# Two cross-attention layers on one Trainium2 core: units of 256 queries, keys and values projected once per batch, layer 1 fourteen groups behind

## What is computed

```python
# layer 0: text tokens 0..1019, image tokens 1020..1023
q = heads(x @ W_q)
k_t, v_t = heads(text @ W_k), heads(text @ W_v)
probs_t = softmax(q @ k_t.T * scale)
text_out = probs_t @ v_t
attn_scores = q @ heads(ip @ W_k_ip).T * scale
qsem = l2norm(probs_t @ text)              # 512 columns for every head
sem = qsem @ l2norm(ip).T
probs_ip = softmax(attn_scores + 0.5 * sem) * spatial_mask
x1 = (text_out + probs_ip @ v_ip) @ W_out + b_out + x

# layer 1: text tokens 0..76, image tokens 77..1023
out = (attend(q, text) + attend(q, image)) @ Wo + bo + x1
```

## Time and profile before

| | us |
|---|---|
| median of three runs | 3646.74 (3644.2 to 3650.6) |
| the profiled execution's own time | 3650.53 |
| its span, first to last instruction | 3648.7 |
| TensorE busy (matmuls) | 3440.8 |
| VectorE, ScalarE, GpSimd busy | 2018.2, 1638.5, 824.4 |
| mean granted TensorE clock | 0.975 |

### The profile page before, as it was taken

The page is one execution under the profiler, slowest core; times in us unless marked ns, Lnnn a source line. Parts: engine busy times, 40 slices in busy tenths (PEclk is TensorE's granted clock), DMA queues, the critical chain, the costliest instruction groups (busy, mean ns, idle before and its releaser), DMA issues.

```text
span 3648.7 us, 58131 instructions
## 1 busy us (share of the span) xinstructions
PE 3440.8 (94%) x21896; PEld 2650.6 (73%) x21896; DVE 2018.2 (55%) x4648; ACT 1638.5 (45%) x3628; POOL 824.4 (23%) x648
## 2 busy tenths in 40 slices
PE   6999999999999999999999999999999999877887
PEld 3788999997888887777777777777688877633333
DVE  4544444453444455655555565655555565656986
ACT  0233434442332345444454454444444554534876
POOL 2111000101101122222222221212221121234665
PEclk8999999999999999999999999999999999988999
DMA  4220111112252111131451111213143111139221
GB/s 157 56 82 25 50 35 28 36 27 82 53 63 71 45 52 50 33 93 36 59 98 43 46 48 50 52 32 88 39 53 37 26 32 33 25 99 79 55 52 33
DMA packets 391741, 196.67 MB, mean 54 GB/s; under 512 B 296972, under 2 KB 355164, under 8 KB 391458
## 3 DMA queue, kind: packets, MB, share of 16 engines
q1 hardware_dynamic: 391464, 192.96, 24.8%
HBM read 136.68 MB, written 55.44 MB: 53 GB/s over the span
## 4 chain that ended last, share of the span: by engine, by line
PE 81%; DVE 6%; ACT 5%; DMA 3%; issue 2%; POOL 2%; SPq 1%; POOLq 0%; ACTq 0%; DVEq 0%
PE acc L783 9%; PE acc L776 9%; PE acc L778 8%; PE acc L779 8%; PE acc L784 8%; PE acc L777 7%; PE av L817 3%; PE spare L853 3%; ACT prob L958 2%; PE spare L817 2%; PE acc L810 2%; PE acc L808 2%; PE score L741 2%; PE score L736 2%; PE score L743 2%
## 5 line engine op out<-in xcount | busy, mean ns | idle before, releaser
L958 ACT ACTIVATE prob<-score 128x512 f32<-128x512 f32 x1280 | 799.4, 625 | 1642.4 <-PE score L743 1241.7
L776 PE MATMUL acc<-tok_v,prob_hi 128*128 128x300 f32 x2240 | 873.4, 390 | 11.8 <-DVE v_f L1083 3.7
L961 ACT ACTIVATE prob_hi<-score 128x512 fp32r<-128x512 f32 x1280 | 799.9, 625 | 0.0
L783 PE MATMUL acc<-tok_v,prob_lo 128*128 128x278 f32 (+1 forms) x2560 | 746.9, 292 | 7.3 <-DVE prob_lo L1021 7.3
L778 PE MATMUL acc<-tok_lo,prob_hi 128*128 128x256 f32 (+1 forms) x2560 | 742.5, 290 | 0.0
L779 PE MATMUL acc<-tok_lo,prob_hi 128*128 128x256 f32 (+1 forms) x2560 | 720.5, 281 | 0.0
L784 PE MATMUL acc<-tok_v,prob_lo 128*128 128x256 f32 (+1 forms) x2560 | 719.5, 281 | 0.0
L1021 DVE TENSOR_TENSOR prob_lo<-prob,prob_hi 128x512 fp32r<-128x512 f32 x880 | 653.0, 743 | 96.7 <-ACT prob_hi L961 95.7
L1255 POOL TENSOR_TENSOR prob_lo<-prob,prob_hi 128x512 fp32r<-128x512 f32 x400 | 529.9, 1338 | 730.5 <-ACT prob_hi L961 729.5
L777 PE MATMUL acc<-tok_v,prob_hi 128*128 128x256 f32 x2240 | 629.2, 281 | 0.0
L778 PEld LDWEIGHTS acc<-tok_lo,prob_hi 128*128 128x128 f32 (+1 forms) x2560 | 485.3, 190 | 10.4 <-issue 9.6
(11 more groups left out here) (221 smaller groups left out, 4438.9 us busy)
## 6 DMA issues: line engine op xcount, KB each, us to landing
k_ring<-k_scr SPq DMA_DIRECT2D x480, 64.0 KB
ctx_t<-in_ctxT SPq DMA_DIRECT2D x8, 2048.0 KB, 10.8
q_ring<-q_scr SPq DMA_DIRECT2D x480, 32.0 KB
v_scr<-v_stage SPq DMA_DIRECT2D x32, 440.0 KB, 2.5
tok_v<-v_scr SPq DMA_DIRECT2D x80, 176.0 KB, 3.3
k_scr<-part_bf SPq DMA_DIRECT2D x32, 384.0 KB, 2.5
v_scr<-v_stage SPq DMA_DIRECT2D x36, 330.0 KB, 9.2
v_ring<-v_scr SPq DMA_DIRECT2D x80, 148.5 KB, 3.3
```

Source lines behind the costliest of these rows:

```text
L776: e.matmul(out_a[:, 0:SEG + VCOLS], p_hi, tok_v[0:kk, c, seg, v_lo:v_lo + SEG + VCOLS], start=first, stop=False)
L783: e.matmul(out_a[:, v_one:v_one + SEG + VH], p_lo, tok_v[0:kk, c, seg, v_lo + v_one:v_lo + v_one + SEG + VH], start=False, stop=False)
L958: e.activation(prob[:, es, :], bank_s[:, :], ACT.Exp, scale=SCALE)
L961: e.activation(prob_hi[:, ps, :], bank_s[:, :], ACT.Exp, scale=SCALE).then_inc(s_exp, 1)
```

## The change

A batch's 512 queries are cut in two units of 256 (PARTS = 2), in both layers: 16 units, 160 groups of 8 chunks. A chunk is 256 keys by 256 queries in both layers. Keys and values are projected once per batch by `project_kv`, a job of its own beside the jobs of the queries (`project_q`); `job_tasks` keeps one job of each kind under way. LAYER_LAG is 14 of the smaller groups. The tiles of the closing get memory of their own. The constants of order (LOOK_LOAD 3, LOOK_MAX 2, AHEAD 3, RING 4, the DMAs of a group) stay.

```diff
-LAYER_LAG = 17
+LAYER_LAG = 14
-B, SQ, D, E, T = 4, 512, 320, 512, 1024
+BATCHES, PARTS = 4, 2
+B, SQ, D, E, T = BATCHES * PARTS, 512 // PARTS, 320, 512, 1024
-PER_GROUP = GROUP * NT
+UNIT_KEYS = 2
+NU = NT // UNIT_KEYS
+PER_GROUP = GROUP * NU
...
-    def project(u):
+    def project_q(u):
         def loads():
-            o.note["loads", u] = (done["x_in"], done["w"], done["ctx"], tuple(done["xout"]))
-            o.add("loads", u)
+            o.note["q_loads", u] = (done["x_in"], tuple(done["xout"]))
+            o.add("q_loads", u)
...
+        return [loads] + [(NM, q_task(m)) for m in range(NM)]
+
+    def project_kv(u):
+        layer = UNITS[u][0]
+
+        def loads():
+            o.note["kv_loads", u] = (done["w"], done["ctx"])
+            o.add("kv_loads", u)
+        tasks = [loads]
...
         for m in range(NM):
-            tasks.append((NM, q_task(m)))
             tasks += [(NE * (1 + (half == (0 if layer else 1))), k_task(m, half)) for half in range(2)]
...
         if layer == 0:
-            add_job(rest + project(B + b), place[(B + b, 0)] - LOOK_LOAD)
+            add_job(rest + project_q(B + b), place[(B + b, 0)] - LOOK_LOAD)
             if b + 2 < B:
-                add_job(project(u + 2), place[(u + 2, 0)] - LOOK_LOAD)
+                add_job(project_q(b + 2), place[(b + 2, 0)] - LOOK_LOAD)
+            if b % PARTS == 1 and b + 3 < B:
+                add_job(project_kv(b + 3), place[(b + 3, 0)] - LOOK_LOAD, "kv")
+            if b % PARTS == 0 and b + 2 < B:
+                add_job(project_kv(B + b + 2), place[(B + b + 2, 0)] - LOOK_LOAD, "kv")
...
         while jobs and (quota > 0 or min(jobs, key=lambda x: x[0])[0] <= g):
-            if under_way and under_way[0] in jobs:
-                job = under_way[0]
-            else:
-                job = min(jobs, key=lambda x: x[0])
-                under_way[:] = [job]
+            first = {}
+            for x in sorted(jobs, key=lambda x: x[0]):
+                first.setdefault(x[2], under_way.get(x[2], x))
+            job = min(first.values(), key=lambda x: x[0])
+            under_way[job[2]] = job
...
-        slots = PER_GROUP * ST - 4 if layer == 0 else PER_GROUP
+        slots = PER_GROUP * 2 * UNIT_KEYS - 4 if layer == 0 else PER_GROUP
...
-                    if UNITS[u][0] == 1:
-                        e.matmul(score[n % 2][:, :], k_ring[0:depth, slot, j, c * P:(c + 1) * P],
-                                 q_ring[0:depth, slot, j, :], start=True, stop=True).then_inc(s_score, 1)
...
+                    queries = q_ring[0:depth, slot, j, :]
+                    e.matmul(score[n % 2][:, 0:SQ], k_ring[0:depth, slot, j, 2 * c * P:(2 * c + 1) * P],
+                             queries, start=True, stop=True)
+                    e.matmul(score[n % 2][:, SQ:2 * SQ], k_ring[0:depth, slot, j, (2 * c + 1) * P:(2 * c + 2) * P],
+                             queries, start=True, stop=True).then_inc(s_score, 1)
...
-                    e.matmul(both[0:n_out, :], weights, prob_hi[:, ps, :], start=first, stop=False, skip_group_check=not first)
+                    for k in range(UNIT_KEYS):
+                        e.matmul(both[0:n_out[k], 0:SQ], weights[k], prob_hi[:, ps, queries[k]],
+                                 start=r == 0 and k == 0, stop=False, skip_group_check=r > 0 or k > 0)
                     e.wait_ge(s_low[on_pool[n]], low_nth[n])
-                    e.matmul(both[0:n_out, :], weights, prob_lo[:, ps, :], start=False, stop=first or last, skip_group_check=not first).then_inc(s_main, 1)
+                    for k in range(UNIT_KEYS):
+                        mm = e.matmul(both[0:n_out[k], 0:SQ], weights[k], prob_lo[:, ps, queries[k]], start=False,
+                                      stop=r == 0 and k == 0 or r == NU - 1 and k == 1, skip_group_check=r > 0 or k > 0)
+                    mm.then_inc(s_main, 1)
...
+        FUSED, TURNED = HS * IP, NM * SQ
+        closing = sb("closing", [P, FUSED + SQ + 2 * TURNED])
```

More of the change, by code:

```diff
@@ L95, in plan @@
     groups = len(seq)
-    chunks = [(g, u, gi * GROUP + j, c) for g, (u, gi) in enumerate(seq) for j in range(GROUP) for c in range(NT)]
+    chunks = [(g, u, gi * GROUP + j, c) for g, (u, gi) in enumerate(seq) for j in range(GROUP) for c in range(NU)]
     now = [0]
     later, urgent, bgq, current = deque(), deque(), deque(), []
-    done = dict(part=[0, 0], splits=0, vst=0, xout=[0, 0], ctx=-1, x_in=-1, w=-1)
+    done = dict(part=[0, 0], splits=0, vst=0, xout=[0] * NM, ctx=-1, x_in=-1, w=-1)
     def settle():
@@ L114, in lower @@
             done["part"][i % 2] += 1
-            o.note["qk", u, m] = tuple(done["part"])
+            o.note[key[0] + "_split", u, m] = tuple(done["part"])
         later.append((now[0] + 2, lower))
-    def project(u):
-        layer, b = UNITS[u]
-        tasks = []
+    def project_q(u):
         def loads():
-            o.note["loads", u] = (done["x_in"], done["w"], done["ctx"], tuple(done["xout"]))
-            o.add("loads", u)
-        tasks.append(loads)
+            o.note["q_loads", u] = (done["x_in"], tuple(done["xout"]))
+            o.add("q_loads", u)
         def q_task(m):
@@ L239, in residual @@
         def residual(m):
-            settle()
-            o.note["residual", u, m] = (done["part"][m % 2], tuple(done["xout"]))
             o.add("residual", u, m)
-        tasks += [lambda: residual(0), lambda: residual(1)]
+        tasks += [lambda m=m: residual(m) for m in range(NM)]
         tasks += [(ST + 1 if layer == 0 else 1, turn(m)) for m in range(NM)]
@@ L254, in go @@
                         yield
[L255 to L258, removed]
+                done["xout"][m] += 1
             return go
@@ L297, in turn_head @@
         o.add("turn_head", u, h)
-    first_unit = project(0)
-    first_loads, first_qk, first_v_loads, *first_v = (first_unit[0], first_unit[1:1 + 3 * NM], *first_unit[1 + 3 * NM:])
+    q_loads, *first_q = project_q(0)
+    kv_loads, *first_kv = project_kv(0)
+    first_k, first_v_loads, first_v = first_kv[:2 * NM], first_kv[2 * NM], first_kv[2 * NM + 1:]
+    first_qk = [t for m in range(NM) for t in (first_q[m], first_k[2 * m], first_k[2 * m + 1])]
     o.add("row_const")
-    first_loads()
+    q_loads()
+    kv_loads()
     o.add("row_scr")
@@ L344, in job_tasks @@
         total, rate = 0, 0
-        for d, tasks in sorted(jobs, key=lambda x: x[0]):
+        for d, tasks, _ in sorted(jobs, key=lambda x: x[0]):
             total += steps_of(tasks)
@@ L642, in cross_attention_pair @@
         s_iprep = sem("ip_rep_done")
-        unit_nth = {s[1]: i for i, s in enumerate([s for s in o.steps if s[0] == "loads"])}
+        unit_nth = {s[1]: i for i, s in enumerate([s for s in o.steps if s[0] == "q_loads"])}
+        kv_unit_nth = {s[1]: i for i, s in enumerate([s for s in o.steps if s[0] == "kv_loads"])}
         v_unit_nth = {s[1]: i for i, s in enumerate([s for s in o.steps if s[0] == "v_loads"])}
@@ L937, in _ @@
                         bank_free(*key)
-                    mm = e.matmul(bank[bank_of[key]][0:w, :], w_o[layer][0:MW[k], k, P * m:P * m + w], o_t[0:MW[k], k, :],
+                    mm = e.matmul(bank[bank_of[key]][0:w, 0:SQ], w_o[layer][0:MW[k], k, P * m:P * m + w], o_t[0:MW[k], k, :],
                                   start=(k == 0), stop=(k == NM - 1))
@@ L1428, in _ @@
             e.wait_ge(s_vout[1], 16 * (stored // 2))
-            e.wait_ge(s_xout[0], 16 * 2 * 2 * B)
-            e.wait_ge(s_xout[1], 16 * 1 * 2 * B)
+            for m in range(NM):
+                e.wait_ge(s_xout[m], 16 * 2 * B)
 def kernel(**inputs):
```

299 lines of the change are left out of this document (144 added, 155 removed).

## The result

The changed kernel takes 3881.2 us (median of 4 runs, 3870.4 to 3882.2) where the kernel before, beside it, takes 3645.5 us (3642.6 to 3650.6). The ratio is 1.0637, 95% interval 1.0618 to 1.0657. The forecast had the direction, 3710 us; the increase is 236 us in place of 63 and ends outside the range.

The account below looks back on a forecast made before the run. TensorE's written order was taken to bound most of the kernel, with idle to win only in the last stage; -70 there and added costs summed to +63 us, giving 3710 us, range 3590 to 3810.

Parts of the forecast that it names:

- Keys right behind their loads: Key projection: first key matmul waits for its context loads, 7 times 3 us, +21 us (0 to +70).
- loads of x and w_q: Query projection: 8 more such loads with q behind each, 3 us each, +24 us (0 to +60).
- Layer 1 alone: Last stage: 488 us shrinks to 192, with 12 us per half group that has loads, set by SP's issues.
- Changes of layer: Pairs: 43 more changes from layer 0 to layer 1, 0.73 us each waiting for ScalarE's squares, +31 us.
- 12 matmuls hide: Pairs: the other change of layer waits on copies that 12 matmuls cover; up to +5 us.
- Smaller matmuls: Layer 1: 640 more score and 1280 more product matmuls, 9 ns each, +17 us (0 to +23).
- Maxima's rows: 80 more tasks for rows of maxima, 0.3 us each with the transpose outside the last stage, +24 us (+8 to +50).
- The start: Before the first product: fewer matmuls of maxima and half of q, -4 us (-10 to 0).
- SP in the pairs, rival two: Pairs: layer 0's key and query loads come 2 to 4 us late in 66 pairs, +150, 3860 us; chance 0.12.
- VectorE as the bound: Rival for layer 1 in the pairs: VectorE limits, +1 us per half group, 3776 us; chance 0.06.
- the last stage and what moved: Shorter last stage against work moved into the pairs: balance -70 us (bounds -115 and -40).
- the forecast's 15 for closings: Unit ends: 8 more closings with as many dependent VectorE steps each, +15 us (+5 to +40).

Follow-up runs that it names:

- e4: Changed kernel without rewriting the key ring's constant rows where the slot's last group had the same layer; 3867.0 us, ratio 1.0611 to the kernel before.
- e3: Changed kernel with a group's value loads issued ahead of its key and query loads; 3892.1 us, ratio 1.0685 to the kernel before.
- e2: Changed kernel with half groups taken two of a layer at a time; 3882.4 us, ratio 1.0653 to the kernel before.
- e7: Kernel before with groups taken two of a layer at a time; 3713.7 us, ratio 1.0182 to the unedited kernel before.
- e9: Changed kernel where layer 1's first product waits only for the squares of the bank it writes; 3867.8 us, ratio 1.0585 to the kernel before.
- e8: Kernel before with layer 1's score and value matmuls of 512 columns each split in two of 256; 3649.3 us, ratio 1.0008.
- e1: Changed kernel with query, key and value jobs' tasks held until the next group once their loads are given out; 3759.8 us, ratio 1.0324.

## Why the prediction was wrong, by its steps

**Keys right behind their loads, +21, and loads of x and w_q, +24: the step that failed.** The trace has 59 and 46 us of waits more (104 before rounding), and what the hold gives back, stalls and slow clock and all, is 114. The mechanism was named and its place was right; the size was taken as 3 us a time where the keys stood up to 13.7 and the queries 9.6. I had the rows for it: the context's landing of 10.8 us was put down as "3 us each" because rows of maxima might stand between, and the 6.2 us of ring issues were counted for the last stage but not for the loads in the pairs, that stand behind them on the same queue. A half group of 8 us can't cover 7 us of issues and 10 of landing, 11 with `w_ip`. The upper bounds, 60 and 70, did hold the waits.

**The clock was left out.** The granted clock fell in the stalls and was at its lower level right behind them (1783.8 to 1797.5 us for the stall shown, which ends at 1793.25). The time at the lower level went from 185 to 338 us, and between the start and layer 1 alone it more than tripled, from 73 to 228. TensorE's busy time rose by 74 us for the same columns, and the hold alone gave 24 of them back. The forecast counted the clock for the last stage only.

**Layer 1 alone, 192.** It took 231. A half group with loads took 14.4 us (ten of them, 11.7 to 16.2) in place of 12: SP's stores of rows wait for the maxima of the group, and so its issues do not follow each other without a gap. TensorE's largest waits there are for VectorE's last maximum ahead of the transpose (24.4 us in 12 times) and for values (13.8 in 5). e4 shows that of issues saved there about half counts, e3 that the order of them gives little. Closing and q took 39.4 us in one half group where 32 were put.

**Changes of layer, +31.** A quiet half group of layer 0 is 2.6 us over columns alone and 3.8 in a pair, a whole one of before 5.2 and 6.5: 1.2 to 1.3 for a change, 52 to 56 for 43 more, so 20 too few. The squares are 0.73 of it; that "12 matmuls hide" the other change was wrong by half a microsecond. So the price is there, and the experiments (e2, e7, e9) say that little of it can be had.

**Smaller matmuls, +17:** 3 (e8). **Maxima's rows, +24:** 19 by the waits. **The start, -4:** -4. **SP in the pairs, rival two:** in the pairs TensorE waits 7 us ahead of the matmuls of maxima, none of it for `q_ring`, so it did not come about in the form told. In e3, with the issues a microsecond later, three such waits for the queries are there (5.5 us). **VectorE as the bound:** only when layer 1 follows itself (e7).

Put together: -31 for the last stage and what moved, +54 changes, +3, +19, +114 behind loads, the forecast's 15 for closings, and -4: 170 of the profile's 231 us. The 15 was not measured, and the 54 is taken from quiet half groups. The other 60 no run takes apart, and they stay open. By e1's page, where the stalls behind loads are gone, TensorE is still idle 59 us longer than before and busy 50 us longer, for 5 us more of columns.

## What to carry to other kernels

When groups are halved, everything that a group must cover keeps its length: write down for each load the issues ahead of it on its queue plus its landing, and compare that with the new group's time, not the old one's. A planner that hands out a job's loads and its first task in one group is safe only while the group is longer than that sum. Holding the tasks for one group gave 114 us here, and nothing in the kernel before, whose groups are twice as long. Before taking out a change between two kinds of work, ask which engine catches up during the other kind.

## What the hardware showed that was not expected

- A stall costs more than itself, but not much more. The half group with 13.7 us of stall was 18.7 us longer than a quiet one of 8.2; 3.4 of the other 5 are columns of its key matmuls, which leaves 1.6 for the lower clock and the rest. Over the kernel it was 24 us of busy time on 98 of idle (e1).
- 1920 matmuls more of half the columns cost 0 to 6 us.
- An issue of 16 KB of queries took 0.42 us on SP, as one of 32 KB had, and six issues of maxima's rows 3.7 us for half the rows that took 4.0 before: in these sizes SP's time goes by the number of transfers and hardly by their size. The 64 KB of keys took 0.42 us too (median of 960); the 0.32 of the earlier trace rows is the first issue of its group. The Trainium skill (DMA: Bandwidth & Descriptors, Measured) has transfers under 64 KB dominated by their descriptors. That is of the transfer itself, measured with transfers issued from GpSimd, and not of the queue's time for an issue, so these figures agree with it in kind only. ACT's queue took 0.33 to 0.61 us for an issue of the query loads in the timeline above.
- The context's 2 MB landed in 9.7 us from SP's queue, behind its other loads, and in 12.0 from ACT's queue, beside them (medians of 8).
